# A graph network on one core: neighbour sums from y kept as high and low parts, one fp32r matmul per edge tile, GpSimd and VectorE written out in full

## The reference

```python
def _sage_conv(x, src, tgt, W_l, b_l, W_r):
    msgs = x[src]
    agg = jax.ops.segment_sum(msgs, tgt, num_segments=n)
    deg = jax.ops.segment_sum(jnp.ones((src.shape[0],), x.dtype), tgt, num_segments=n)
    agg = agg / jnp.maximum(deg, 1.0)[:, None]
    return agg @ W_l + b_l + x @ W_r
```

## Time and profile before

| what | us |
|---|---|
| median of 3 runs (4266.0 to 4267.86) | 4267.46 |
| the profiled execution's own time | 4262.32 |
| its span | 4260.5 |
| POOL busy, share of the span | 1935.2 (45%) |
| PE busy | 2569.0 (60%) |
| DVE busy | 1849.4 (43%) |
| gathers of both neighbour stages (L1415), busy / idle just before | 879.6 / 457.5 |

### The profile page before, as it was taken

One profiled execution on the slowest core, in us unless ns is written; L12 is line 12 of the kernel. 1 busy time (PEld: TensorE's weight loads), 2 busy tenths in 40 slices (PEclk: granted clock), 3 DMA queues, 4 the chain that ended last, 5 costly groups with the idle time before them and its releaser, 6 DMA issues. The chain is left out here.

```text
span 4260.5 us, 47165 instructions
## 1 busy us (share of the span) xinstructions
PE 2569.0 (60%) x9048; PEld 1655.4 (39%) x9049; DVE 1849.4 (43%) x4308; ACT 1032.5 (24%) x2880; POOL 1935.2 (45%) x1900
## 2 busy tenths in 40 slices
PE   0121113866888888888797965555555555545398
PEld 0000001222555555555575643333333333333266
DVE  9500002556667766666222642222223322222479
ACT  0011112757545544444212220000000000000032
POOL 3877773000444444444111004666664566666520
PEclk9965556988899999999898987667666776766599
DMA  3111111113444444444532124333335333333521
GB/s 124 41 27 32 31 30 37 59 66 116 127 130 137 134 133 137 131 126 130 123 100 64 59 70 134 97 95 95 96 95 86 116 98 96 96 94 96 101 71 37
DMA packets 247793, 390.83 MB, mean 92 GB/s; under 512 B 82663, under 2 KB 169322, under 8 KB 246829
## 3 DMA queue, kind: packets, MB, share of 16 engines
q0 software_dynamic: 94976, 250.63, 21.5%
q1 hardware_dynamic: 129802, 110.65, 8.3%
q10 hardware_dynamic: 22948, 28.86, 2.2%
HBM read 308.20 MB, written 67.78 MB: 88 GB/s over the span
## 5 line engine op out<-in xcount | busy, mean ns | idle before, releaser
L1415 POOL DMA_INDIRECT nbr_yg<-y_d,nbr_idx x928 | 879.6, 948 | 457.5 <-issue 253.4
L1492 PE MATMUL nbr_sum<-nbr_yg,nbr_hot 128*128 128x258 f32 x1856 | 672.6, 512 | 640.2 <-issue 285.4
L1492 PEld LDWEIGHTS nbr_sum<-nbr_yg,nbr_hot 128*128 128x128 f32 x1856 | 439.4, 253 | 864.2 <-issue 544.0
L629 POOL DMA_INDIRECT qg<-q_d,rb x464 | 463.4, 999 | 529.7 <-DVE hb L744 445.8
L1454 DVE TENSOR_TENSOR nbr<-nbr_sum,nbr 128x258 f32 x464 | 197.5, 426 | 1018.5 <-remote 534.6
L299 POOL DMA_INDIRECT recs_d<-stage,stage_pos x416 | 454.0, 1091 | 177.5 <-issue 130.3
L492 PE MATMUL acc<-col_hot,lane_hot 128*128 128x464 f16 x832 | 244.9, 414 | 415.9 <-ACT lane_hot L325 277.4
L777 PE MATMUL p_h<-p_hl,trs 128*128 x928 | 338.6, 448 | 74.4 <-ACT trs L662 37.6
L325 ACT ACTIVATE lane_hot<-lane_one,val 128x128 f16<-128x128 f16 x832 | 255.8, 388 | 456.0 <-issue 327.7
L744 DVE TENSOR_TENSOR hb<-p_h,qg 128x512 f32<-128x512 f32 x464 | 301.2, 683 | 109.2 <-PE p_h L780 94.7
L457 DVE TENSOR_SCALAR lane_one<-iota_b,lane 128x128 f16<-128x128 f16 x416 | 107.0, 257 | 524.7 <-remote 338.7
(11 more groups left out here) (257 smaller groups left out, 4054.9 us busy)
## 6 DMA issues: line engine op xcount, KB each, us to landing
nbr_yg<-y_d,nbr_idx POOLq DMA_INDIRECT x928
recs_d<-fill SPq DMA_DIRECT2D x16, 493.0 KB, 14.4
rb<-recs_d SPq DMA_DIRECT2D x58, 136.0 KB
qg<-q_d,rb POOLq DMA_INDIRECT x464
stage<-recs SPq DMA_DIRECT2D x52, 136.0 KB
recs_d<-stage,stage_pos POOLq DMA_INDIRECT x416
q_d<-q_out ACTq DMA_DIRECT2D x25, 256.0 KB
p_d<-p_out ACTq DMA_DIRECT2D x25, 256.0 KB
```

Of the source, the lines that this page charges most:

```text
L629: pool.indirect_dma_start(qg[r][:, :], None, S.q[:, :], bass.IndirectOffsetOnAxis(ap=rb[b][:, r // 2, at:at + 1].bitcast(U32), axis=0)).th ...
L1415: pool.indirect_dma_start(yg[t][:, 0:D], None, S.y[:, :], bass.IndirectOffsetOnAxis(ap=idx[b][:, r:r + 1], axis=0)).then_inc(s_gath[t], 16)
L1492: last_mm = pe.matmul(p_sum[q % SUMS][:, 0:W], hot[t // HB_T][:, t % HB_T, :], yg[t][:, :], start=(j == 0), stop=(j == 1))
```

## The change

y is stored as two parts of 256 columns each: its value rounded to fp32r, and the remainder. Rows of y in DRAM, gathers, matmuls, PSUM sums and accumulators become 512 columns wide, the matmul's operands become fp32r, and the two halves of a sum are added when it is used. The degree is no longer a column of the gathered tile: in the first layer alone PE multiplies each one-hot matrix by two columns of ones into banks of its own, and DVE adds that to `C.rdeg`, which is inverted once. POOL and DVE of the neighbour stage have no loops any more; PE and ACT keep theirs. The index copies on ACT and the bounds checks of the bucket numbers are gone, and 16 numbers are loaded at a time.

```diff
 stage_project
+        y = m.sb("y", [P, CH, 2, D], F32R)
-        HSTEPS = 3 + CH
+        HSTEPS = 2 + CH
 (ACT, after take_transposed)
+                    wait_past(act, s_y_st, 16 * c)
+                    for t in range(CH):
+                        src = out.to_take(act, c, t)
+                        act.activation(y[:, t, 0, :], src[:, 0:D], ACT.Copy).then_inc(s_high, 1)
 (DVE, second_rows)
-                    dve.tensor_scalar(rdeg[:, :, :], C.nbr[:, bass.ds(c * CH, CH), D:D + 1], 1.0, None, ALU.max).then_inc(s_h, 1)
-                    dve.reciprocal(rdeg[:, :, :], rdeg[:, :, :]).then_inc(s_h, 1)
+                    part = C.nbr[:, bass.ds(c * CH, CH), :, :]
+                    dve.tensor_tensor(h[:, :, :], part[:, :, 0, :], part[:, :, 1, :], ALU.add).then_inc(s_h, 1)
 (DVE, products)
-                        dve.tensor_copy(y[:, t, :], src[:, 0:D]).then_inc(out.empty, 1)
+                        dve.wait_ge(s_high, CH * c + t + 1)
+                        dve.tensor_tensor(y[:, t, 1, :], src[:, 0:D], y[:, t, 0, :].bitcast(F32), ALU.subtract).then_inc(out.empty, 1)
 stage_neighbours
-        SUMS = 4
+        SUMS, LOAD = 4, 16
+        AHEAD = 2 if layer == 0 else SUMS
-        yg = [m.sb(f"yg{b}", [P, W]) for b in range(T)]
+        yg = [m.sb(f"yg{b}", [P, 2 * D], F32R) for b in range(T)]
 (POOL)
-                        pool.wait_ge(s_idx, 2 * i + b + 1)
-                            pool.indirect_dma_start(yg[t][:, 0:D], None, S.y[:, :],
-                                                    bass.IndirectOffsetOnAxis(ap=idx[b][:, r:r + 1], axis=0)
+                for t in range(NCOL):
+                    if t >= T and t % 2 == 0:
+                        pool.wait_ge(s_sum, (t - T) // 2 + 1)
                         pool.nop(nofuse=True)
+                    pool.indirect_dma_start(yg[t % T][:, :].bitcast(F32), None, S.y[:, :],
+                                            bass.IndirectOffsetOnAxis(ap=C.gidx[:, t:t + 1], axis=0)
 (DVE)
+                    if layer == 0:
+                        deg = C.rdeg[:, bass.ds(bucket, 1)]
+                        dve.tensor_tensor(deg, p_deg[g % 2][:, 0:1], deg, ALU.add)
+                    into = C.nbr[:, bass.ds(bucket, 1), :, :].rearrange("p a h n -> p (a h n)")
+                    dve.tensor_tensor(into, p_sum[g % SUMS][:, :], into, ALU.add).then_inc(s_acc, 1)
+                for g in range(NG):
+                    if g % LOAD == 0:
+                        buckets = load_own_buckets(nc, dve, C.bucket[0:1, 1, g:min(g + LOAD, NG)])
+                    accumulate(g, buckets[g % LOAD])
 (PE)
-                            pe.wait_ge(s_acc, G * i + q - SUMS + 1)
+                            pe.wait_ge(s_acc, G * i + q - AHEAD + 1)
+                            if layer == 0:
+                                pe.matmul(p_deg[q % 2][:, 0:2], edges, ones[:, :], start=(j == 0), stop=(j == 1))
-                            last_mm = pe.matmul(p_sum[q % SUMS][:, 0:W], hot[t // HB_T][:, t % HB_T, :], yg[t][:, :],
-                                                start=(j == 0), stop=(j == 1))
+                            last_mm = pe.matmul(p_sum[q % SUMS][:, :], edges, yg[t][:, :], start=(j == 0), stop=(j == 1))
 stage_last (DVE)
-                step.link(dve.tensor_scalar(rdeg[:, :, :], C.nbr[:, :, D:D + 1], 1.0, None, ALU.max))
-                step.link(dve.reciprocal(rdeg[:, :, :], rdeg[:, :, :]))
+                    dve.tensor_tensor(x3[:, :, :], part[:, :, 0, :], part[:, :, 1, :], ALU.add).then_inc(s_x3, 1)
```

More of the change, by code:

```diff
@@ L822, in load_buckets, with load_own_buckets @@
     return nc.values_load_multi_w_load_instructions(ap, engines=[eng.engine], min_val=0, max_val=NT - 1)[1]
+def load_own_buckets(nc, eng, ap):
+    return nc.values_load_multi_w_load_instructions(
+        ap, engines=[eng.engine], min_val=0, max_val=NT - 1,
+        skip_runtime_bounds_check_because="a bucket's number is counted on the chip, one less than at most NT")[1]
 class Banks:
@@ L1402, in _ @@
             def _(pool):
[L1403 to L1407, removed]
-                        pool.wait_ge(s_idx, 2 * i + b + 1)
-                        pool.nop(nofuse=True)
[L1410 to L1414, removed]
-                            pool.indirect_dma_start(yg[t][:, 0:D], None, S.y[:, :],
-                                                    bass.IndirectOffsetOnAxis(ap=idx[b][:, r:r + 1], axis=0)
-                                                    ).then_inc(s_gath[t], 16)
-                bodies(pool, gathers)
+                for t in range(NCOL):
+                    if t >= T and t % 2 == 0:
+                        pool.wait_ge(s_sum, (t - T) // 2 + 1)
+                        pool.nop(nofuse=True)
+                    pool.indirect_dma_start(yg[t % T][:, :].bitcast(F32), None, S.y[:, :],
+                                            bass.IndirectOffsetOnAxis(ap=C.gidx[:, t:t + 1], axis=0)
+                                            ).then_inc(s_gath[t % T], 16)
             @block.scalar
@@ L1423, in _ @@
                 act.sem_inc(s_z_taken, 1)
[L1425 to L1438, removed]
+                with act.Fori(0, NT) as tile:
+                    act.wait_ge(s_z, tile + 1)
+                    act.activation(C.z[:, bass.ds(tile, 1), :].rearrange("p a n -> p (a n)"), p_z[:, 0:D],
+                                   ACT.Copy).then_inc(s_z_taken, 1)
             @block.vector
@@ L1443, in _, with one_hot @@
                 wide = [P, HB_T, P]
-                def one_hot(i, b):
-                    dve.tensor_tensor(hot[b][:, :, :], p_iota[:, :, :].to_broadcast(wide),
-                                      dloc[:, bass.ds(T * i + HB_T * b, HB_T), :].to_broadcast(wide),
+                def one_hot(n):
+                    dve.tensor_tensor(hot[n % 2][:, :, :], p_iota[:, :, :].to_broadcast(wide),
+                                      dloc[:, HB_T * n:HB_T * n + HB_T, :].to_broadcast(wide),
                                       ALU.is_equal).then_inc(s_hot, 1)
[L1450 to L1468, removed]
@@ L1470, in _, with accumulate @@
-                bodies(dve, body)
+                def accumulate(g, bucket):
+                    dve.wait_ge(s_sum, g + 1)
+                    if g > 0:
+                        dve.wait_ge(s_acc, g)
+                    if layer == 0:
[3 more added lines that the diff above has]
+                    dve.tensor_tensor(into, p_sum[g % SUMS][:, :], into, ALU.add).then_inc(s_acc, 1)
@@ new lines, in _ @@
+                dve.memset(C.nbr[:, :, :, :], 0.0).then_inc(s_nbr_zero, 1)
+                dve.wait_ge(s_nbr_zero, 3)
+                half = HB_T // 2
+                for g in range(NG):
+                    if g % LOAD == 0:
+                        buckets = load_own_buckets(nc, dve, C.bucket[0:1, 1, g:min(g + LOAD, NG)])
+                    accumulate(g, buckets[g % LOAD])
+                    n = g // half + 2
+                    if g % half == half - 1 and n * HB_T < NCOL:
+                        one_hot(n)
@@ L1472, in _ @@
+                if layer == 0:
+                    dve.wait_ge(s_acc, NG)
+                    dve.tensor_scalar(C.rdeg[:, :], C.rdeg[:, :], 1.0, None, ALU.max).then_inc(s_deg, 1)
+                    dve.wait_ge(s_deg, 1)
+                    dve.reciprocal(C.rdeg[:, :], C.rdeg[:, :]).then_inc(s_deg, 1)
             @block.tensor
@@ L1474, in _, with body @@
                 pe.wait_ge(s_w, 16)
-                pe.wait_ge(s_zero, T)
-                def body(i, first, last, tile):
+                pe.wait_ge(s_ones, 2)
+                def body(i, first, tile):
                     if tile is not None:
```

94 lines of the change are left out of this document (52 added, 42 removed).

## The result

The changed kernel took 4281.98 us (median of 6 runs, 4275.06 to 4288.62), the kernel before 4266.73 beside it: a ratio of 1.0038, 95% interval 1.0026 to 1.0049. Forecast were 4131 and faster. The profiled execution took 4280.42 us, its span 4278.6.

A forecast was written before the change was run, and what follows sets the result against it. POOL's gathers were taken as the bound, 1.25 us each, 580 us a layer, plus 178 us of stalls. -166 + 10 - 2 + 15 + 7 = -136 from 4262.3, plus 5 to the median, gave 4131 us; range 4095 to 4275.

The forecast's parts named there:

- Step 3: DVE in the neighbour stages: without checked loads and loop steps, stalls fall from 178 to 12 us, -166.
- Step 1: POOL's gather pace in the neighbour stages: unaltered by wider rows or the missing loop, 0, bounds 0 and +47 us.
- Step 2: DMA of the doubled gathers: 210 GB/s at a share of 0.73, hidden behind POOL; +10 us, bounds 0 and +74.
- The tail: End of each neighbour stage: 21 padding gathers at 1.5 us trail POOL by 5 us; +10 for both layers.
- Step 4: PE in the neighbour stages: one 512-column fp32r pass of 0.40 us a tile, hidden behind 1.25 us, worth 0.
- Steps 5 and 6: Neighbour stages' index copies, memsets and earlier first gather, -2 us; projections' extra copies, adds and doubled stores, +15 us.
- The wait for the relu: Second projection: relu starts after ACT's last copy, transposes stand 2 us a chunk, 5 chunks, +10 us.
- DVE is hidden: Second projection: DVE, with a 1.49 us add and two small operations fewer, comes to 7.2 of 9 us.
- Step 7: Last stage: five 128x1280 adds on DVE's path, old reciprocal gone; +7 us, bounds +3 and +15.
- Rival D: Whole kernel: stalls fall by about 30 us, eaten by projection and last stage; 4267 us, chance 0.04.
- B: Neighbour stages: DVE's stretches stay, PE's lead in layer 0 falls from four groups to two; 4337 us, chance 0.11.

The follow-up runs named there:

- a_1kb: The changed kernel with the low half left out of the transfers, so each gather brings 128 rows of 1 KB: 3740.9 us, single run, where before takes near 3705.

## Why the prediction was wrong

- Step 3, the stalls, failed: "So I take the stalls to fall from 178 to 12 us: -166." They fell to 159. The step laid them to DVE's slow sequencer steps around checked loads. Those steps were a symptom: with the checks and loops gone DVE still stands 9.46 us at a time, and with them in place the steps are at most 190 and 33 ns at 3705, and POOL never pauses. The stalls come with POOL's own stream: at 4267 a layer takes 650 us or more, 1.40 us a gather, not 1.25 and 580. The change won 19 us in these stages instead of 166. (The loops have 27 jumps a stage at most, not 28; nothing hangs on that.) The first profile had it to be seen: in the first stage ScalarE did 78 instructions in 250 us beside the scatters and 498 in 250 us right after them:

```profile
400.00:650.00 250.00, 27.36 (x78) 0.53 0.11 29
680.00:930.00 250.00, 153.72 (x498) 0.82 0.15 54
```

- Step 1 held: 0.945 us a gather with rows of 2 KB, the bound of +47 not touched, and a_1kb shows no price of the bytes. So the 51 ns more of the edge network's gathers are not the price of 2 KB rows; what they are was not tried. Step 2 held in kind: at 3705, where POOL gathers every 1.25 us, the share is 0.74 at 211 GB/s, forecast 0.73 at 210. The tail, taken at +10, is small: from the last gather's start to the stage's last instruction 12.4 and 14.7 us after, 11.5 and 12.6 before, +3. Step 4 held, hidden; at 3705 PE waits for gathers, as forecast.
- Steps 5 and 6: the second projection cost 15.9 us and the first 2.1, with 2 us more at the start of each neighbour stage, 22 against 15 - 2 forecast. The wait for the relu came as described, and at its size, 2 us a chunk. What the step lacked is TensorE's clock behind that wait, 5.7 us: its products start 9.4 to 11.8 us apart, not every 9.

```profile
3318.81 1.27 ACT L1308 ACTIVATE project_x<-project_h 128x1280 f32<-128x1280 f32 x1
...
3320.22 0.76 PE L861 MATMUL project_tr<-ident,project_x 128*128 128x128 f32 x5 [1.83 <-ACT project_x L1308]
```

  That DVE is hidden held in this order of ACT's work, and failed once the relu was moved.
- Step 7: 9.2 against 7.
- The remaining account at 4267: 18 more in projections, 4 at starts, 9 in the last stage, 19 less in the neighbour stages make +12; the span grew by 18.1, the rest being that the stages ahead of the first projection, which the change doesn't touch, ended some 6 us later. Rival D, "stalls fall by about 30 us, which the projection and last stage eat", given 0.04, came nearest: they fell by 19, and the other stages cost more than that. B named the right event (the stretches stay) with the wrong mechanism: layer 0, with its lead of two groups, stalls no more than before.

## What to carry to other kernels

Where several engines at once have waits without a named cause, look at what runs unbroken beside them, and at a moment when it stops: that is worth more than the slowest steps of the engine that is late. POOL was busy for 440 of 668 us, and yet its idle time could not be had. Make the suspect slower by a cheap operation: if the total stays, as it did here from 1.25 to 1.44 us a gather, its own pace was not the limit. A wait of 2 us for TensorE can cost more than 2 us, by the clock behind it. Before a gain is built on stalls, see whether another chip has them.

## What was not expected of the hardware

- One program, two levels: 3705 and 4267 us, the whole difference in stages where POOL issues indirect DMAs (up to the edge network's start 358 us, neighbour stages 170, edge network 31, with 948 and 945 ns per gather of the neighbour stages).
- At 4267 the other engines' progress against the step of 128-row indirect DMAs: 76, 222, 334, 533 instructions in 250 us at 1.28, 1.36, 1.47, 1.68 us. Semaphore updates are seen late (8.3 us above) and sequencer steps are longer (1386 against 190 ns); what in the hardware holds both up no run here shows.
- A memset of 64 columns between two gathers adds 0.03 us to the step. One of 256 takes 0.33 us and adds 0.19: 0.14 us of the 0.30 us gap takes in other work.
